# Decoder megakernel: context value products moved into the first stage's last rounds, one convolution product moved to GpSimd, and stage borders thinned

## The chip, the cores and the metric

The program runs on 1 core of one Trainium2 chip. The metric is the device time of one execution in microseconds (us); of several runs the median is taken. The engines are PE (TensorE, matmuls), DVE (VectorE), ACT (ScalarE), POOL (GpSimd) and SP (SyncE, which here only issues DMAs).

## The reference

Two decoder layers on x of 8 batches x 256 tokens x 512 features, with a context of the same shape, all in f32:

```python
x = _layernorm(x + _L0_attn_ref(x, ...), axis=-1)            # differential attention
x = _layernorm(x + _L0_xattn_ref(x, L0_xattn_k, fside_S2_0, ctx_2048, ctx_2048, 8), axis=-1)
x = _layernorm(x + _L0_ffn_ref(x, ...), axis=-1)             # 8 experts, top 2
x = _layernorm(x + _L1_attn_ref(x, ...), axis=-1)
x = _layernorm(x + _L1_xattn_ref(x, mask, ctx_2048, ctx_2048, wq, wk, wv, wo), axis=-1)
x = _layernorm(x + _L1_ffn_ref(x, W_gate, W_qkv), axis=-1)
```

Two pieces matter here. The long convolution of `_L0_xattn_ref` is, for each of the 32 groups of 8 channels, with v = x and x1 = x2 = context:

```python
kv = vr[:, :, :, None, :] * x2r[:, :, None, :, :]
y = jnp.fft.irfft(jnp.fft.rfft(kv, n=fft_size) * k_f[None, :, None, None, :], n=fft_size)[..., :L]
y = y + kv * skip
out = jnp.einsum('bhijl,bhil->bhjl', y, x1r)
```

And `_L1_xattn_ref` attends to the context, whose projections do not depend on x. The kernel folds the weights, so that the context is only multiplied by wq (scaled, "context queries", kept in DRAM as `ctx_q`) and by wo ("context values", `ctx_o`).

## The kernel before

The program is a sequence of stages, each a block with one hand-written instruction list per engine. A stage ends with `Stage.retire` (L44), which clears the stage's semaphores on POOL and puts up a barrier of all engines. Stages named `mid`, `kept` and `const` hold semaphores that live across the others, and each of them retires with a barrier too: `mid` before the last stage, `kept` and `const` at the end of the program. PSUM tiles are handed out in turn by `Banks` (L84): `claim` waits until the tile's turn before was drained, so a claim also waits for whoever drains the tile four turns back (the ring of the first stage has four).

**First stage (`front_stage`, L189).** Layer 0's attention, run as a software pipeline of rounds r = 0 to 11. In a round, batch d = r is projected, a = r-1 has its scores and exponentials, f = r-2 has the last part of its attention weighed, its output projection and norm, and u = r-3 is turned and gets its skip product. Rounds 2 to 8 hold all the work of a and f; in round 8 (a = 7) there is no d left, in round 9 (f = 7) no a either. PE's list is at L409 to L480. The score tiles (six `S` for the maxima, L310 to L330, six `T` for the exponentials, L344) share one buffer of four banks, so a score waits for the reader before it. The end of a round on the others:

- ACT (L671 to L681) takes the last exponential `exps(a, 5)`, copies the sums `take_sums(a, 1, 0)` (L607), and then makes `squares(a, 0)` (L611 and L612).
- POOL (L563 to L565) masks the last exponential tile (`causal(a, 5)`, L543, an affine select of 128x2048) and then adds the two squares (`add_eps(a, 0)`, L549), for which PE's `square_sums` (L380) of the next round waits.
- DVE's `combine(a, 1, 0)` (L720 to L725) needs ACT's sums; its last two operations read SBUF alone. After it come the maxima of the next round (`maxima`, L695), each of which releases PE's next score.

SP loads the inputs, stores `base` after each batch and, when T scores of batch 6 are made, loads the first two filters.

**Convolution (`long_conv_stage`, L893).** 32 groups h. POOL makes kv for the four chunks of 128 positions and the sum of the first two (L960, L958), into one of two buffers; it starts on h once PE has done with h-2. PE makes 9 products of 128x512 (L937), in f32, into 5 of 8 banks. DVE weighs the results with the context and sums over i: chunks 0 and 1 out of PSUM (L998), chunks 2 and 3 first completed with the shared part (L1004) and then, in SBUF, multiplied by the context (L1022); `sums` (L1009) reduces them two chunks at a time.

**Middle (`middle_stage`, L1033).** Norm, router, folding of weights, then routing on DVE (a long chain of small operations, in two pieces: up to the picks, and from the counts of L1182 to `hot_ready`), with PE filling the time with context products: for each batch `ctx_queries` (L1146) and `ctx_values` (L1154), batches 0 to 5. The counts come after batch 0's, the matmuls that make the token list (L1193) after batch 2's. After these POOL gathers the first two token tiles (L1246). ACT copies each result and stores it.

**Experts (`experts_stage`, L1411).** 39 tiles of 128 tokens: transpose (L1451), gate and up (L1456), silu, product, transpose, down (L1483), store. The first tile is transposed and copied (L1535) at the start. ACT ends by waiting for its stores, since the last stage gathers from them.

**Last stage (`tail_stage`).** Layer 1. It begins with the context products of batches 6 and 7.

## Time and profile before

| what | value |
|---|---|
| median of 3 runs | 2226.31 us (2226.2 to 2229.31) |
| the profiled execution, its own time | 2224.11 us |
| its span, first to last instruction | 2222.4 us |
| TensorE's mean granted clock | 0.979 |
| PE busy | 2093.0 us (94%) |
| DVE busy | 1250.0 us (56%) |
| POOL busy | 541.8 us (24%) |
| ACT busy | 516.3 us (23%) |
| DMA moved | 129.57 MB, 58 GB/s over the span |

Busy is the time in which an engine works on an instruction. Matmuls overlap, so the time that one matmul costs in a row of them is the distance of their starts. Where an engine idles, a row of the timeline tells how long and who released it.

### The profile page before, as it was taken

How to read it: one execution, taken by the hardware profiler on the slowest of the kernel's cores; microseconds unless marked ns; L12 is line 12 of the kernel's file. 1: busy time of each engine (PE TensorE's matmuls, PEld its weight loads, DVE VectorE, ACT ScalarE, POOL GpSimd, SP SyncE). 2: the span in 40 equal slices, each digit the busy share in tenths (PEclk: the TensorE clock that was granted, in tenths of full speed). 3: DMA queues.
4: the chain of work that ended last, by engine and by line, in shares of the span. 5: the costliest groups of instructions: out<-in, count | busy, mean ns of one | idle time of the engine just before them, and what ended most of it. 6: DMA issues, size and time to landing. Idle time of an engine off the chain costs nothing. (4 is left out here: it accounts for less than half of the span.)

```text
span 2222.4 us, 29341 instructions
## 1 busy us (share of the span) xinstructions
PE 2093.0 (94%) x11935; PEld 1221.2 (55%) x11935; DVE 1250.0 (56%) x1825; ACT 516.3 (23%) x783; POOL 541.8 (24%) x511
## 2 busy tenths in 40 slices
PE   7899999878999899899999898999999999999996
PEld 5444444324444466556665565566666666666654
DVE  2467777666999944022222225365757585847466
ACT  1444444440000121111111121122222222222121
POOL 2122222226777400011111221112121212111111
PEclk9999999989999999999999999999999999999998
DMA  8950000005111145521212412101010101000000
GB/s 171 99 48 29 29 29 20 31 10 200 46 42 42 34 140 190 200 67 62 67 67 67 178 40 96 48 1 48 1 58 1 58 1 39 1 29 11 1 10 20
DMA packets 65649, 129.57 MB, mean 58 GB/s; under 512 B 6416, under 2 KB 19856, under 8 KB 65520
## 3 DMA queue, kind: packets, MB, share of 16 engines
q1 hardware_dynamic: 44864, 75.39, 13.3%
q10 hardware_dynamic: 14976, 33.69, 4.2%
q0 software_dynamic: 5680, 18.62, 2.8%
q8 instruction: 99, 1.62, 0.3%
q14 instruction: 30, 0.25, 0.0%
HBM read 96.36 MB, written 41.81 MB: 62 GB/s over the span
## 5 line engine op out<-in xcount | busy, mean ns | idle before, releaser
L937 PE MATMUL conv_conv<-kv,toep 128*128 128x512 f32 x576 | 248.5, 594 | 0.0
L2434 DVE RECIPROCAL tail_inv<-tail_ring 128x256 f32<-128x256 f32 x64 | 112.4, 1756 | 188.7 <-PE tail_ring L1772 181.4
L1456 PE MATMUL moe_gu_ps<-gu,moe_xT 128*128 x624 | 199.0, 462 | 3.9 <-issue 2.3
L937 PEld LDWEIGHTS conv_conv<-kv,toep 128*128 128x128 f32 x576 | 110.0, 191 | 139.0 <-issue 131.6
L960 POOL TENSOR_TENSOR kv<-vT,cT 128x512 f32<-128x512 f32 x128 | 147.2, 1172 | 58.1 <-PE conv_conv L937 53.6
L1456 PEld LDWEIGHTS moe_gu_ps<-gu,moe_xT 128*128 128x128 f32 x624 | 116.0, 191 | 73.0 <-issue 23.6
L2125 POOL TENSOR_TENSOR tail_rstd_x<-tail_rstd_x,const_minus_half 128x2 f32<-128x2 f32 x31 | 21.9, 707 | 499.0 <-DVE tail_rstd_x L2386 499.0
L2132 POOL TENSOR_SCALAR_AFFINE_SELECT tail_expT<-tail_expT 128x1024 f32<-128x1024 f32 x64 | 71.2, 1112 | 237.3 <-ACT tail_expT L2207 237.1
L543 POOL TENSOR_SCALAR_AFFINE_SELECT front_expT<-front_expT 128x2048 f32<-128x2048 f32 x32 | 64.4, 2012 | 256.1 <-ACT front_expT L599 256.1
L1540 DVE TENSOR_TENSOR moe_hid<-moe_gu_ps,moe_silu 128x352 f32<-128x352 f32 x39 | 20.4, 524 | 179.3 <-PE moe_gu_ps L1456 179.3
L599 ACT ACTIVATE front_expT<-front_scores 128x2048 f32<-128x2048 f32 x48 | 90.1, 1878 | 81.1 <-PE front_scores L354 81.1
L2207 ACT ACTIVATE tail_expT<-tail_scores 128x1536 f32<-128x1536 f32 x64 | 92.8, 1450 | 66.3 <-PE tail_scores L1749 66.3
L1437 POOL DMA_INDIRECT xg<-x_after,tokens x37 | 34.9, 945 | 299.2 <-PE moe_xT_ps L1451 299.2
L1483 PE MATMUL moe_y_ps<-down,moe_hT 128*128 (+1 forms) x234 | 107.1, 593 | 0.7 <-ACT moe_hT L1524 0.7
L695 DVE TENSOR_REDUCE front_negtop<-front_scores 128x8 f32<-128x2048 f32 x32 | 73.2, 2288 | 27.8 <-PE front_scores L320 27.8
L2420 DVE TENSOR_TENSOR tail_allowed<-tail_scores,const_mask_bf 128x1024 f32<-128x1024 f32 x48 | 58.5, 1218 | 46.8 <-PE tail_scores L1724 46.6
L1022 DVE TENSOR_TENSOR total<-total,cT 128x512 f32<-128x512 f32 x62 | 82.8, 1374 | 1.1
L1507 ACT ACTIVATE moe_silu<-moe_gu_ps 128x352 f32<-128x352 f32 x39 | 18.1, 463 | 272.7 <-PE moe_gu_ps L1456 272.7
L2137 POOL TENSOR_TENSOR tail_expT<-tail_expT 128x512 f32<-128x512 f32 x60 | 76.6, 1277 | 5.0
L977 ACT COPY both<-conv_conv 128x512 f32<-128x512 f32 x32 | 18.6, 585 | 230.6 <-PE conv_conv L937 213.1
L1553 DVE COPY moe_y<-moe_y_ps 128x512 f32<-128x512 f32 x39 | 27.0, 691 | 72.4 <-PE moe_y_ps L1483 72.4
L185 PE MATMUL tail_ring<-tail_gk,tail_xT 128*128 128x416 f32 (+1 forms) x256 | 63.4, 399 | 3.3 <-ACT tail_xT L2190 3.3
(372 smaller groups left out, 4006.0 us busy)
## 6 DMA issues: line engine op xcount, KB each, us to landing
toep<-toeplitz SPq DMA_DIRECT2D x32, 320.0 KB, 2.9
y_slots<-moe_y ACTq DMA_DIRECT2D x39, 256.0 KB, 2.0
gu<-in_L_ffn_gate_up_proj SPq DMA_DIRECT2D x5, 1408.0 KB, 11.2
toeplitz<-filt_rows SPq DMA_DIRECT2D x1, 6144.0 KB, 66.7
front_e<-in_ctx SPq DMA_DIRECT2D x8, 512.0 KB, 5.5
toeplitz<-filt_rows SPq DMA_DIRECT2D x2, 2048.0 KB, 88.5
x_after<-x SPq DMA_DIRECT2D x8, 512.0 KB, 5.1
tail_x<-x_after SPq DMA_DIRECT2D x8, 512.0 KB, 4.0
```

Of the source, the lines that this page charges most:

```text
L543: pool.affine_select(out=tile, in_=tile, compare_op=ALU.is_ge, fill=0.0, base=0, pattern=[[0, 16], [1, P]], channel_multiplier=-1).then_in ...
L599: act.activation(exp_buf(b, n)[:].rearrange("p g j q -> p g (j q)"), scores[:], ACT.Exp).then_inc(quads.drained_sem(key), 1)
L695: ins = dve.tensor_reduce(negtop[:, 1, n].rearrange("p (g a) -> p g a", a=2), scores[:].rearrange("p g (a k) -> p g a k", a=2), AX_X, ALU. ...
L937: ins = pe.matmul(bank, toep[p][:, mat * P:(mat + 1) * P], kv[p][:, c].rearrange("p b j i -> p (b j i)"), start=n == 0, stop=n == len(PART ...
L960: pool.tensor_tensor(kv[p][:, c], tokens_of(c, h), context_of(c, h, 3), ALU.mult).then_inc(kv_ready, 1)
L1022: ins = dve.tensor_tensor(total[:, lc - 2], total[:, lc - 2], context_of(lc, h, 2), ALU.mult)
L1456: ins = pe.matmul(gu_ps[:, s % 2, h, 0:HID], xT[:, c, :], wgu[c][:, e, h * HID:(h + 1) * HID], start=c == 0, stop=c == NC - 1)
L1483: ins = pe.matmul(y_ps[:, s % 2, :], hT[0:w, n, :], wd[n][0:w, e, :], start=n == 0, stop=n == 2)
L2132: pool.affine_select(out=diagonal, in_=diagonal, compare_op=ALU.is_ge, fill=0.0, base=0, pattern=[[0, 8], [1, P]], channel_multiplier=-1). ...
L2137: pool.tensor_tensor(e[:, 3], e[:, 0], e[:, 2], ALU.add).then_inc(masked[kind], 1)
L2207: act.activation(exp_buf(kind, b, c)[:, 0:3].rearrange("p n g q -> p g n q"), scores[:, :, 0:3 * P].rearrange("p g (n q) -> p g n q", q=P) ...
L2434: link.after(dve.reciprocal(inv[c % 2][:], bank[:, S:2 * S]))
```

## The change

It has five parts.

1. **Context values of batches 0 to 2** leave the middle stage and are made in the first stage's rounds 8 and 9. There are six groups of four f32 products: batch 0 and the first half of batch 1 in round 8, the rest in round 9. Their weights (wo, 1 MB) are loaded by SP into `wq`, once the last query is projected; ACT copies and stores the results.
2. **Order in the first stage**, in every round: ACT squares before it copies the last sums; POOL adds before it masks the last tile; PE turns the context in two halves.
3. **Convolution**: POOL multiplies chunk 3 by the context (`weigh_last`), two groups late. DVE reduces chunk 2 and chunk 3 apart, chunk 3 one group late.
4. **First expert tile**: it is transposed in the middle stage, between the context queries and the context values of batch 5.
5. **Borders**: `mid`, `kept` and `const` retire without a barrier, and the wait for the experts' stores goes from ACT, ahead of the barrier, to POOL, behind it.

```diff
+        if not self.lasts:
+            self.nc.all_engine_barrier()
...
+                def ctx_values(b, t, parts=(0, 1)):
+                    key = ("ctxo", b, t)
+                    if 0 in parts:
+                        pe.wait_ge(ctx_wo_loaded, 16)
+                        ring.claim(pe, key)
+                    for c in range(NC // 2 * parts[0], NC // 2 * (parts[-1] + 1)):
+                        ins = pe.matmul(ring.tile(key), cT[:, b, c, t * P:(t + 1) * P], wide["wq"][:, c, :], start=c == 0, stop=c == NC - 1,
+                                        skip_group_check=True)
...
                         score(a, 0)
+                        if a == B - 1: ctx_values(0, 0, (0,))
                         if f is not None: square_sums(f, 0)
+                        if a == B - 1: ctx_values(0, 0, (1,))
...
-                        if f is not None: weigh(f, 1, 1, ("O",))
+                        if f is not None:
+                            weigh(f, 1, 1, ("O",))
+                            turn_context(f, 0)
...
-                            turn_context(f)
+                            turn_context(f, 1)
...
                         if u is not None: turn_tokens(u)
+                        if a == B - 1: ctx_values(0, 1, (0,))
...
                         if f is not None: square_sums(f, 1)
+                        if a == B - 1: ctx_values(0, 1, (1,))
                         score(a, 5)
+                        if a == B - 1: ctx_values(1, 0)
...
+                        ctx_values(1, 1)
                         weigh(f, 1, 1)
                         square_sums(f, 0)
                         turn_tokens(u)
+                        ctx_values(2, 0)
                         square_sums(f, 1)
                         octets(u)
                         for t in range(NT):
                             out(f, t)
+                        ctx_values(2, 1)
...
                     if a is not None:
+                        add_eps(a, 0)
                         causal(a, 5)
-                        add_eps(a, 0)
...
                     if a is None and u is not None:
                         for n in range(2):
                             take(("x1", u, n), vT[:, 2 * n:2 * n + 2, u, :])
+                    if a is None and f is not None: take_ctx_values(2, 0)
...
                         exps(a, 5)
+                        squares(a, 0)
                         take_sums(a, 1, 0)
-                        squares(a, 0)
...
+                def weigh_last(h):
+                    pool.wait_ge(ring.drained_sem((h, 3)), ring.count((h, 3)))
+                    pool.tensor_tensor(final[h % 2][:, 0], final[h % 2][:, 0], context_of(3, h, 2), ALU.mult).then_inc(weighed, 1)
...
+                        if h >= 2 and c == K01:
+                            weigh_last(h - 2)
+                weigh_last(H - 2)
...
+                    completed(h, 2)
+                    completed(h, 3)
+                    weighted_full(h, 2)
+                    sums(h, 2, total[:])
+                    if h:
+                        dve.wait_ge(weighed, h)
+                        sums(h - 1, 3, final[(h - 1) % 2][:])
+                weighted_full(H - 1, 3)
+                sums(H - 1, 3, final[(H - 1) % 2][:])
...
+                    if b == B - 3:
+                        pe.wait_ge(mid.gathered[0], 16)
+                        bank = ring.claim(pe, "tile")
...
+                    if b >= EARLY:
+                        ctx_values(b)
...
-                for p in range(2):
-                    act.wait_ge(y_stored[p], 16 * len(range(p, TILES, 2)))
...
+                for p in range(2):
+                    pool.wait_ge(y_stored[p], 16 * len(range(p, TILES, 2)))
                 fetch(0)
```

**Order on ScalarE, the end of a round of the first stage** (`expT` exponentials, `sums` the copied sums, `zz` and `square` the squares). Before:

```order
L599 ACTIVATE front_expT<-front_scores 128x2048 x2
L607 COPY front_sums<-front_ring 128x512
L599 ACTIVATE front_expT<-front_scores 128x2048
L607 COPY front_sums<-front_ring 128x512
L611 ACTIVATE front_zz<-front_zz 128x512
L612 ACTIVATE front_square<-front_am 128x512
```

Now:

```order
L627 ACTIVATE front_expT<-front_scores 128x2048 x2
L635 COPY front_sums<-front_ring 128x512
L627 ACTIVATE front_expT<-front_scores 128x2048
L651 ACTIVATE front_zz<-front_zz 128x512
L652 ACTIVATE front_square<-front_am 128x512
L635 COPY front_sums<-front_ring 128x512
```

The copy of the sums, for which DVE's combination waits, now stands behind both squares.

**Order on TensorE, from the end of round 8 into round 9** (`expT` with `v` and `ones` are the weighing, `front_e` is the turned context, `kept_wa` holds a batch of x that is turned, `front_wq` holds wo by then). Before:

```order
L373 MATMUL front_ring<-front_expT,front_v 32x512 x4
L373 MATMUL front_ring<-front_expT,front_ones 32x512 x4
L289 MATMUL front_ring<-const_ident,front_e 128x128 x8
L373 MATMUL front_ring<-front_expT,front_v 32x512 x8
L373 MATMUL front_ring<-front_expT,front_ones 32x512 x8
L380 MATMUL front_ring<-front_square,const_strips 128x512
L289 MATMUL front_ring<-const_ident,kept_wa 128x128 x8
L380 MATMUL front_ring<-front_square,const_strips 128x512
L394 MATMUL front_ring<-front_skipped,const_octets 128x512 x2
L387 MATMUL front_ring<-front_wo,front_am 128x512 x8
```

Now:

```order
L376 MATMUL front_ring<-front_expT,front_v 32x512 x4
L376 MATMUL front_ring<-front_expT,front_ones 32x512 x4
L292 MATMUL front_ring<-const_ident,front_e 128x128 x8
L406 MATMUL front_ring<-front_wq,cT 128x512 x4
L376 MATMUL front_ring<-front_expT,front_v 32x512 x8
L376 MATMUL front_ring<-front_expT,front_ones 32x512 x8
L383 MATMUL front_ring<-front_square,const_strips 128x512
L292 MATMUL front_ring<-const_ident,kept_wa 128x128 x8
L406 MATMUL front_ring<-front_wq,cT 128x512 x4
L383 MATMUL front_ring<-front_square,const_strips 128x512
L397 MATMUL front_ring<-front_skipped,const_octets 128x512 x2
L390 MATMUL front_ring<-front_wo,front_am 128x512 x8
```

One group of context values stands ahead of the weighing of f = 7, one ahead of its second square sums.

**Order on TensorE in the middle stage, behind the last logits** (`midl_ring<-cT,plain_wq` queries, `raw_wo,cT` values, `marked` the token list). Before:

```order
L1146 MATMUL midl_ring<-cT,plain_wq 128x256 x16
L1154 MATMUL midl_ring<-raw_wo,cT 128x512 x8
L1182 MATMUL midl_count_ps<-m,earlier 128x128
L1182 MATMUL midl_count_ps<-m,ones 128x128
L1146 MATMUL midl_ring<-cT,plain_wq 128x256 x16
L1154 MATMUL midl_ring<-raw_wo,cT 128x512 x8
L1146 MATMUL midl_ring<-cT,plain_wq 128x256 x16
L1154 MATMUL midl_ring<-raw_wo,cT 128x512 x8
L1193 MATMUL midl_ring<-marked,at_lane 128x78 x32
L1146 MATMUL midl_ring<-cT,plain_wq 128x256 x16
L1154 MATMUL midl_ring<-raw_wo,cT 128x512 x8
L1146 MATMUL midl_ring<-cT,plain_wq 128x256 x16
```

Now:

```order
L1215 MATMUL midl_ring<-cT,plain_wq 128x256 x16
L1250 MATMUL midl_count_ps<-m,earlier 128x128
L1250 MATMUL midl_count_ps<-m,ones 128x128
L1215 MATMUL midl_ring<-cT,plain_wq 128x256 x48
L1223 MATMUL midl_ring<-raw_wo,cT 128x512 x8
L1268 MATMUL midl_ring<-marked,at_lane 128x78 x32
L1215 MATMUL midl_ring<-cT,plain_wq 128x256 x16
L1223 MATMUL midl_ring<-raw_wo,cT 128x512 x8
L1215 MATMUL midl_ring<-cT,plain_wq 128x256 x16
L1259 MATMUL midl_ring<-const_ident,xg_73 128x128 x4
L1223 MATMUL midl_ring<-raw_wo,cT 128x512 x8
```

Three pairs of value groups are gone; the counts stand behind one batch of queries, the token list behind 4 of queries and 1 of values; the transposes of the first tile (`xg`) come before the last values.

## Rows read from the trace of the kernel before

**Rows 1.** Engines by stretch (us, busy (x instructions), clock): a round, last rounds, convolution
```profile
253.00:309.00 56.00, 53.91 (x368) 26.38 (x368) 39.73 (x48) 26.64 (x36) 11.50 (x8) 1.00 0.09 29
...
421.00:478.00 57.00, 46.80 (x300) 17.25 (x300) 35.94 (x42) 20.28 (x23) 10.37 (x7) 0.91 0.03 10
...
514.00:768.00 254.00, 248.57 (x577) 109.69 (x575) 241.65 (x259) 18.62 (x32) 183.10 (x157) 0.99 0.22 73
```

**Rows 2.** Timeline of TensorE in the middle stage: start us, us, what [idle before]
```profile
842.75 7.03 PE L1154 MATMUL midl_ring<-raw_wo,cT 128*128 128x512 f32 x16
849.62 0.38 PE L1182 MATMUL midl_count_ps<-m,earlier 128*128 128x128 f32 x2
...
913.32 7.03 PE L1154 MATMUL midl_ring<-raw_wo,cT 128*128 128x512 f32 x16
```

**Rows 3.** Timeline of TensorE and VectorE where the expert stage begins
```profile
922.83 1.09 PE L1451 MATMUL moe_xT_ps<-const_ident,xg 128*128 128x128 f32 x4 [2.48 <-PEq L52]
926.20 6.54 PE L1456 MATMUL moe_gu_ps<-gu,moe_xT 128*128 x16 [2.29 <-issue]
...
932.86 0.53 DVE L1540 TENSOR_TENSOR moe_hid<-moe_gu_ps,moe_silu 128x352 f32<-128x352 f32 x1 [8.22 <-PE moe_gu_ps L1456]
```

**Rows 4.** Landing of the gathers, from the view of tile xg
```profile
DMA to landing us min/median/max: 3.2/3.3/8.1
```

**Rows 5.** Timelines of ScalarE, GpSimd, VectorE, TensorE where round 6 begins
```profile
306.30 0.59 ACT L607 COPY front_sums<-front_ring 128x512 f32<-128x512 f32 x1
...
308.32 1.43 POOL L549 TENSOR_TENSOR front_square<-front_square,front_zz 128x512 f32<-128x512 f32 x1
...
308.55 1.48 DVE L725 SCALAR_TENSOR_TENSOR front_am<-front_cross,front_lam 128x256 f32<-128x256 f32 x1
309.96 2.28 DVE L695 TENSOR_REDUCE front_negtop<-front_scores 128x8 f32<-128x2048 f32 x1
...
309.80 1.12 PE L380 MATMUL front_ring<-front_square,const_strips 128*128 128x512 f32 x2 [1.10 <-POOL front_square L549]
...
316.65 0.61 PE L316 MATMUL front_scores<-const_mask_bf,const_ident_bf 128*128 128x256 bf16 x4 [0.63 <-DVE front_negtop L695]
```

**Rows 6.** Timeline of TensorE in round 9 and into the convolution
```profile
480.46 1.92 PE L373 MATMUL front_ring<-front_expT,front_v 128*32 128x512 f32 x16 [2.30 <-DVE front_cross L722]
...
490.10 2.08 PE L380 MATMUL front_ring<-front_square,const_strips 128*128 128x512 f32 x2 [3.74 <-POOL front_square L549]
...
507.06 1.97 PE L289 MATMUL front_ring<-const_ident,kept_wvo 128*128 128x128 f32 x8 [4.41 <-DVE kept_wvo L783]
510.53 3.75 PE L928 MATMUL conv_conv<-front_e,const_octets 128*128 128x512 f32 x4 [1.50 <-PEq L52]
```

**Rows 7.** Timelines of GpSimd and VectorE, end of round 8; all of L725
```profile
476.09 2.24 POOL L543 TENSOR_SCALAR_AFFINE_SELECT front_expT<-front_expT 128x2048 f32<-128x2048 f32 x1
...
476.39 2.22 DVE L725 SCALAR_TENSOR_TENSOR front_am<-front_cross,front_lam 128x256 f32<-128x256 f32 x1
...
L725 DVE SCALAR_TENSOR_TENSOR front_am<-front_cross,front_lam x32: 471/478/2223, 72.1 to 486.0; 128x256 f32<-128x256 f32 x32
```

**Rows 8.** Convolution: three operations by line; timelines of GpSimd (608) and VectorE (767)
```profile
L960 POOL TENSOR_TENSOR kv<-vT,cT x128: 1062/1067/2049, 510.5 to 751.6; 128x512 f32<-128x512 f32 x128
...
L958 POOL TENSOR_TENSOR kv<-kv x32: 1263/1271/1276, 512.7 to 749.4; 128x512 f32<-128x512 f32 x32
...
L1022 DVE TENSOR_TENSOR total<-total,cT x62: 677/1328/1554, 529.2 to 759.2; 128x512 f32<-128x512 f32 x62
...
608.15 2.09 POOL L960 TENSOR_TENSOR kv<-vT,cT 128x512 f32<-128x512 f32 x2 [1.79 <-PE conv_conv L937]
...
767.01 0.69 DVE L1009 TENSOR_REDUCE vT<-total 128x64 f32<-128x512 f32 x1
```

**Rows 9.** Timeline of TensorE where the last stage begins
```profile
1249.60 0.67 PE L1846 MATMUL tail_ring<-cT,plain_wq 128*128 128x256 f32 x2 [4.00 <-PEq L52]
```

**Rows 10.** Timeline of SyncE's queue at the end
```profile
2217.29 1.34 SPq L2107 DMA_DIRECT2D out_x<-tail_x  x2
```

149 lines of the change are left out of this document (91 added, 58 removed).

## The prediction

> **What bounds the kernel now.** I read the page first: PE is busy for 94% of the span and heads the chain that ended last, so a microsecond counts only if it lies on PE's path. The engines by stretch then show where PE is the limit [rows 1]. A round of the first stage takes 56 us, PE is busy for 53.91 of them. In the last rounds it idles for 10.2 of 57 us at a granted clock of 0.91. In the convolution it is busy for 248.57 of 254 us; DVE has 241.65 and POOL 183.10. A group there is 248.5 / 32 = 7.77 us of PE work. The middle stage and the experts run without PE idle in a row of matmuls. So three things can move the time: products that PE no longer makes in a full stretch, PE's idle at a border or a late round, and another engine that becomes the bound. The rest is hidden.
>
> All sums are against the profiled execution, 2224.11 us. It lies 2.2 us below the median of 2226.31 us, and I add these 2.2 us at the end.
>
> **(a) Three batches of values out of the middle.** 16 recorded matmuls take 7.03 us, and the next work begins 849.62 - 842.75 = 6.87 us after the first of them [rows 2]. PE is full there, so 3 x 6.87 = 20.6 us go. What could give some back: the routing chain on DVE and the gathers run behind this work. The counts now come behind one batch of queries, without the 6.87 us of values, so the routing starts earlier by that. From counts to token list there were four pieces of 6.87 us before (two batches of queries and values) and there are four now. From the list to the first use of the gathered tile three pieces remain, 20.6 us, and the slowest gather took 8.1 us to land [rows 4]. So: -20.6.
>
> **(b) First expert tile.** Before, the last values ended at 913.32 + 6.87 = 920.2 us and the first gate matmul began at 926.20: 6.0 us, made of a border (2.48), 1.09 of transposes and 2.29 of waiting for their copy and the expert's number [rows 3]. Now the transposes stand in the middle stage: two 128x128 matmuls took 0.38 [rows 2], so four of two passes about 0.7. The border of 2.5 stays, and I leave 1.4 of the 2.29, since the number must still be read. That is 4.6 us against 6.0: -1.4. The SiLU waits for the last store of context results, which hardly moves towards it: its product began right behind the up matmuls at 932.86 [rows 3], so little slack is there. Bounds: 0 and -3.4.
>
> **(c) The order in rounds 2 to 7.** ACT now squares first, POOL adds first. The add began at 308.32 and PE's square sums at 309.80, after 1.10 us of idle [rows 5]. With the squares ahead of the copy (0.59), and the add ahead of the select (2.24 [rows 7]), this idle goes. But DVE's combination waits for the copy, which comes later by two squares, about twice 0.6, as the copy itself (0.59) has as many elements: 1.2 us. It then meets POOL's select instead of the shorter add. What that does rows 7 show: beside a select of 2.24 us the last operation of the combination took 2.22 us, against a median of 0.478. Beside the add of 1.43 us it took 1.48 [rows 5]: it ends some 0.28 us behind POOL's operation both times (310.03 against 309.75; 478.61 against 478.33). I place the new select at about 308.7 to 310.7, so the combination ends at 311.3 and the maxima at 311.3 + 2.28 = 313.6, where they ended at 309.96 + 2.28 = 312.24. The next score waits for them (PE idled 0.63 for the same reason at 316.65 [rows 5]). Of the 1.3 us the earlier square sums and the halved turning of the context absorb part; I take +0.8 a round, +4.8 for six rounds. Bounds: -6.6 (the idle of 1.10 goes, nothing comes) and +9 (1.5 a round).
>
> The Trainium skill (SBUF — State Buffer, "SBUF: two separate sides") says that GpSimd and VectorE share a port pair under an exclusive lock, held for the whole instruction. By that rule alone the delay would be the select's rest, up to 2.2 us a round, or +13; without it the step would bring -6.6. The stretched operations of rows 5 and 7 agree with it.
>
> **(d) Rounds 8, 9 and the convolution's start.** Six value groups of 3.44 us (half of 6.87) enter, 20.6 us of work. Three go into round 8, where PE idles for 10.2 us [rows 1]: their 10.3 us fill the idle, and some slow matmuls there run at full clock: -1.3. In round 9 (1,1) goes ahead of the weighing, whose start waited 2.30 for DVE, and delays it by about 2.4, since its tile was only just drained by then. (2,0) lies in the 3.74 of idle before the second square sums at 490.10 [rows 6], but ACT takes (2,0) ahead of the squares. With the 2.4 this moves the square sums to about 494.8, +4.65. What stands behind them (2.08 in rows 6, then octets and output projection) runs at a higher clock, which I put at -1.15: the norm ends +3.5 later. (2,1) lies in the 4.41 us of idle ahead of the last turning. That turning took 1.97 for 8, though 8 of the same shape take half of that at full clock, the four of L928 took 3.75 where full clock needs about half [rows 6], and the first products were slow too: 1.0 + 1.8 + 1.1 = 3.9 come back. Together -1.3 + 3.5 - 3.9 = -1.7. This is my least certain term: bounds -8 (the moved sums cost nothing, and the clock is back) and +6 (ACT's delay and the 2.4 in full, no clock). Loading wo (1 MB) and ACT's extra stores lie beside this, where SP and ACT idle, and cost nothing.
>
> **(e) The convolution.** PE's 32 x 7.77 us stay. DVE loses a product of 1.33 us median a group [rows 8], which shortens an engine that was hidden. POOL idled 1.79 us before a group [rows 8]. Its new weighing is not in the trace; nearest are its products of the same size in two groups of lines, 1.067 us (L960) and 1.27 us (L958, all in SBUF), the longest 2.05. I take 1.27, as its input too was just written in place: POOL has 7.73 - 1.79 + 1.27 = 7.2 us in a group of 7.73 and stays hidden, with 0.5 us left. Only at the end, where DVE drains behind PE, one product less counts, less a sum (0.69) that now stands apart: -0.8.
>
> The Trainium skill (Perfetto Trace Analysis, "Optimizing Scalar/DVE Operations") warns that moving work between GpSimd and DVE may not help, for their shared port. By it the 1.33 us are not gained; here they aren't counted anyway. The spread of L1022 (0.68 to 1.55) [rows 8] agrees.
>
> **(f) Experts to the last stage.** PE begins at 1249.60 after 4.00 us [rows 9], against 2.48 at the border before the experts [rows 3]. The difference, 1.5, is the wait for the stores, which POOL now takes while PE starts its own context work; the barrier of `mid` goes too, 0.6 at least: -2.1. Bounds -3 and 0.
>
> **(g) The end.** `kept` and `const` retire without a barrier. The last store was issued by 2217.29 + 1.34 = 2218.6 [rows 10], the span ends at 2222.4; landing takes about 2 of these 3.8 us (the page's median for the experts' stores). Two barriers can be 0 to 2: -1.0.
>
> **The sum:** -20.6 - 1.4 + 4.8 - 1.7 - 0.8 - 2.1 - 1.0 = -22.8, so 2224.11 - 22.8 = 2201.3, and 2203.5 for the median.
>
> **The rivals.**
> 1. The order in the rounds helps: the combination isn't caught, and 1.10 goes in each of six rounds, -6.6 in place of +4.8: about 2192. For it speaks PE's idle before the square sums, against it both stretched rows. 0.12.
> 2. The last rounds cost more: (d) at +6 in place of -1.7, as ACT's copies delay squares, every tile of the ring of four waits for its drain, and the moved groups delay PE instead of filling its idle: 7.7 more, about 2211. For it speaks that ACT and DVE, not PE, set round 9. 0.15.
> 3. The middle gives back 5 us, because gathers or expert weights are late: about 2208.5. Against it stand 20.6 us of cover over 8.1. 0.07.
> 4. The other side: POOL becomes the bound of the convolution. The weighing would have to exceed 1.79 us to bind at all; to make up for 22.8 us and 4.5 more, the group must grow by 27.3 / 31 = 0.88 us, so the weighing must take over 2.67 us. By the longest row, 2.05, it costs only 0.26 x 31 = 8 us (2211.5). At 3.0 us, if each weighing waits in full for a DVE product and each DVE product for POOL, it is 1.21 x 31 = 37 us: 2241, slower than before. For it: both engines would be busy for nearly the whole group. Against: the median of L960 is its minimum nearly, although DVE is 95% busy beside it. 0.04.
>
> **How the numbers follow.** Forecast 0.62, rivals 0.12, 0.15, 0.07, 0.04. The range goes from 2195 (three quarters of the way to rival 1) to 2211 (rival 2). A measurement of this kernel can tell about 0.2%, 4.5 us, from no change. Faster by more: all but rival 4 and a tail, 0.94; within 0.2%: 0.03; slower: 0.03.
>
> **What the profile would show.** (a) PE's middle stage shorter by 20 us and without new idle before the transposes. (b) The first gate matmul about 4.6 us behind the last values. (c) Rounds of 56.8 us, combinations stretched to some 2 us, no idle before the square sums and more before the next score; rounds of 55 would prove me wrong. (d) Clock near 1 from round 8 on, idle before the second square sums of round 9. (e) 32 groups of 7.7 us, POOL busy for 7.2 of them, with idle for PE; if POOL has none, rival 4 holds. (f), (g) PE's first matmul of the last stage some 2.5 us behind the experts, and a shorter end. A time above 2211 or below 2195 would say that a step is missing.

## Result and the profile after

The changed kernel takes 2205.7 us (2201.74 to 2211.74, 4 runs) against 2227.74 us for the kernel before (2226.2 to 2229.31, 4 runs): a ratio of 0.9902, 95% interval 0.9881 to 0.9923. That is 22.0 us less, where 22.8 were forecast, and the time lies in the range. The near hit hides errors that cancel, though, as the stretches show. In a second set of runs the same kernel had a median of 2209.39 (2202.33 to 2214.41, 6 runs) and the kernel before 2227.01 (2219.94 to 2231.49, 11 runs): 17.6 us less there, and either kernel moves by some 12 us between executions.

The page's busy line of after:

```profile
PE 2088.7 (95%) x11935; PEld 1215.9 (55%) x11935; DVE 1203.7 (55%) x1825; ACT 516.0 (23%) x783; POOL 578.7 (26%) x542
```

TensorE is busy for 4.3 us less (it has the same products to make) and its mean granted clock is 0.984 (0.979 before); VectorE's work fell by 46 us and GpSimd's grew by 37.

The profiled execution after is 2205.38 us, its span 2203.6, which is 18.8 less than before. I cut both spans at the same seven places of TensorE's timeline (start of the first square sums of round 2, of round 7, of the first convolution product, the first matmul of the middle stage, the first context queries, the first gate matmul, the first matmul of the last stage):

| stretch | before | after | difference | forecast |
|---|---|---|---|---|
| start to the square sums of round 2 | 84.85 | 79.49 | -5.36 | -1.1 |
| five rounds | 280.84 | 288.78 | +7.94 | +4.0 |
| rounds 7 to 9, to the convolution | 148.39 | 153.56 | +5.17 | +0.2 |
| convolution and its border | 254.34 | 252.05 | -2.29 | -0.8 |
| middle, up to the queries | 67.34 | 66.99 | -0.35 | 0 |
| queries to the first gate matmul | 90.44 | 68.42 | -22.02 | -22.0 |
| experts and their border | 323.40 | 322.16 | -1.24 | -2.1 |
| last stage to the end | 972.80 | 972.15 | -0.65 | -1.0 |

(The forecasts are the terms of the prediction by stretch; the square sums come 1.1 earlier in their round, which is -1.1 in the first row and comes back in the third.) The first row is no effect of the change: of the 14 profiles of this study, before's among them, the granted clock of the first 80 us is 0.89 in six and 0.96 in eight, with kernels of the old and of the changed order in either group, and the square sums of round 2 come at 84.1 to 85.4 or at 79.0 to 81.3 us.

The routing and middle stage, columns as in [rows 2]: TensorE's timeline after.

```profile
847.86 0.38 PE L1250 MATMUL midl_count_ps<-m,earlier 128*128 128x128 f32 x2
...
897.83 0.60 PE L1259 MATMUL midl_ring<-const_ident,xg 128*128 128x128 f32 x4
898.27 7.03 PE L1223 MATMUL midl_ring<-raw_wo,cT 128*128 128x512 f32 x16
909.29 3.29 PE L1540 MATMUL moe_gu_ps<-gu,xT_tile 128*128 x5 [3.99 <-issue]
```

No matmul of the middle stage waits for the routing, and the transposes of the first tile have no idle ahead of them: the three batches of values ([rows 2]) are gone in full. The gate begins 909.29 - (898.27 + 6.87) = 4.15 us behind the last values, where it was 6.0. But its first 16 matmuls took 7.42 us here and 6.54 before ([rows 3]): TensorE's idle is now one piece of 3.99 us, and from 909 to 912 us the granted clock was 0.50. In a second profile of the same kernel (e0 below) they took 6.69 us. So 0.9 us of the 1.4 gained at this border went to the clock in this profile, which is most of why the experts' row has -1.24 and not -2.1.

A round of the first stage, the one that answers to [rows 5]: TensorE, then VectorE, GpSimd and ScalarE.

```profile
253.52 1.10 PE L383 MATMUL front_ring<-front_square,const_strips 128*128 128x512 f32 x2
...
258.25 0.61 PE L319 MATMUL front_scores<-const_mask_bf,const_ident_bf 128*128 128x256 bf16 x4 [1.91 <-DVE front_negtop L743]
258.79 2.09 PE L323 MATMUL front_scores<-front_kT,front_qT 32*128 32x512 f32 x8
260.80 2.62 PE L376 MATMUL front_ring<-front_expT,front_v 128*32 128x512 f32 x16
...
253.41 2.19 DVE L772 TENSOR_TENSOR front_zz<-front_sums 128x256 f32<-128x256 f32 x1
255.91 2.28 DVE L743 TENSOR_REDUCE front_negtop<-front_scores 128x8 f32<-128x2048 f32 x1
...
252.09 1.27 POOL L577 TENSOR_TENSOR front_square<-front_square,front_zz 128x512 f32<-128x512 f32 x1 [5.69 <-ACT front_square L652]
253.31 2.00 POOL L571 TENSOR_SCALAR_AFFINE_SELECT front_expT<-front_expT 128x2048 f32<-128x2048 f32 x1
...
251.91 0.58 ACT L635 COPY front_sums<-front_ring 128x512 f32<-128x512 f32 x1
```

ScalarE's copy of the sums now ends at 252.49. GpSimd's select began at 253.31 and ended at 255.31. VectorE's multiplication of the sums (L772, SBUF alone), which takes 0.426 us at the median, took 2.19 and ended at 255.60, 0.29 behind it: it is the forecast pile-up, one operation earlier than placed. Without it the combination would have ended 1.8 us sooner, so the select, and not the later copy alone, makes it late. The maxima then end at 258.19, and PE, which before had idled 1.10 and 0.63 us in two places [rows 5], idles 1.91 in one. Behind that idle the next matmuls are slow: L323 took 2.09 us here, 1.14 one score later.

The granted clock of that place, in the engines by stretch (as in [rows 1]: the stretch, its length, then busy time of PE, its weight loads, VectorE, ScalarE and GpSimd, the granted clock, and DMA share and GB/s):

```profile
256.00:259.00 3.00, 1.09 (x10) 0.53 (x12) 3.00 (x2) 0.38 (x1) 0.00 (x0) 0.97 0.00 0
259.00:262.00 3.00, 3.00 (x16) 0.70 (x20) 1.86 (x2) 0.00 (x0) 0.00 (x0) 0.50 0.00 0
...
314.00:317.00 3.00, 1.09 (x10) 0.46 (x11) 3.00 (x3) 0.38 (x1) 0.00 (x0) 1.00 0.00 0
317.00:320.00 3.00, 3.00 (x26) 0.81 (x27) 2.78 (x2) 0.00 (x0) 0.00 (x0) 1.00 0.00 0
```

In the first of the two rounds the clock was granted at 0.50 for three microseconds (1.2 GHz), right after the idle; in the next round the same idle left it at 1.00. A round with the fall lasted 58.09 us (253.52 to 311.61), one without it 56.66, before 55.89. So the order, with the halved turning, costs 0.77 a round, as forecast (0.8), and where the clock falls another 1.43, which was not forecast.

The last rounds, answering to [rows 6], TensorE, ScalarE, and the engines by stretch:

```profile
482.72 3.67 PE L406 MATMUL front_ring<-front_wq,cT 128*128 128x512 f32 x8 [1.40 <-DVE front_cross L770]
492.07 3.60 PE L406 MATMUL front_ring<-front_wq,cT 128*128 128x512 f32 x8
498.80 2.08 PE L383 MATMUL front_ring<-front_square,const_strips 128*128 128x512 f32 x2 [3.12 <-POOL front_square L577]
515.79 1.09 PE L292 MATMUL front_ring<-const_ident,kept_wvo 128*128 128x128 f32 x8 [0.98 <-DVE kept_wvo L831]
518.43 3.56 PE L980 MATMUL conv_conv<-front_e,const_octets 128*128 128x512 f32 x4 [1.55 <-PEq L52]
...
495.77 0.60 ACT L602 ACTIVATE front_xT<-front_ring 128x512 f32<-128x512 f32 x1 [2.21 <-PE front_ring L406]
496.26 0.62 ACT L651 ACTIVATE front_zz<-front_zz 128x512 f32<-128x512 f32 x1
...
511.00:514.00 3.00, 3.00 (x8) 1.33 (x7) 2.39 (x7) 0.00 (x0) 0.01 (x1) 1.00 0.00 0
519.00:522.00 3.00, 3.00 (x5) 1.18 (x4) 0.69 (x1) 0.00 (x0) 2.92 (x4) 0.56 0.66 195
```

ScalarE's squares (from 496.26) stood behind its copy of the values (2,0) (495.77), which waits for PE to finish that group at 495.7. The second square sums then waited 3.12 us for GpSimd, and behind this idle they ran at the lower clock (2.08 us for a pair that takes 1.12 in round 9's first sums). So did the round's octets right behind them (3.62 for 4; 1.88 in e2 below, where the idle is gone). The output projection ran at full clock but for its start (7.29 for 16, 7.13 in e2), and the clock stood at 1.00 until the convolution's border. There it fell anew: the convolution's octets took 3.56 for 4. In e0, the same kernel with the same waits (3.13 and 1.55), they took 1.95 at full clock:

```profile
521.45 1.95 PE L980 MATMUL conv_conv<-front_e,const_octets 128*128 128x512 f32 x4 [1.55 <-PEq L52]
```

So the octets' slowness is not the square sums' doing, and why it comes in one execution and not in the other is open. The products behind the octets did get faster, as forecast: the first twelve came within 6.44 us here and 7.57 before, a gain of 1.1 us that lies in the convolution's row of the table.

GpSimd's weighing (L1005) and products in the convolution, by line (ns: least, median, most), answering to [rows 8]:

```profile
L1005 POOL TENSOR_TENSOR final<-final,cT x31: 1260/1267/1649, 537.0 to 762.3; 128x512 f32<-128x512 f32 x31
L1016 POOL TENSOR_TENSOR kv<-vT,cT x128: 1055/1066/2047, 518.4 to 759.9; 128x512 f32<-128x512 f32 x128
```

And the timeline of GpSimd in one group, of TensorE at the two borders and of SyncE at the end ([rows 8, 9, 10]):

```profile
630.22 2.53 POOL L1016 TENSOR_TENSOR kv<-vT,cT 128x512 f32<-128x512 f32 x2 [0.57 <-PE conv_conv L989]
634.06 1.27 POOL L1005 TENSOR_TENSOR final<-final,cT 128x512 f32<-128x512 f32 x1
...
773.88 3.30 PE L1176 MATMUL midl_ring<-const_ident,vT 128*128 128x128 f32 x16 [4.69 <-PEq L52]
...
1231.45 4.73 PE L1927 MATMUL tail_ring<-cT,plain_wq 128*128 128x256 f32 x13 [1.92 <-PEq L52]
...
2199.16 1.33 SPq L2188 DMA_DIRECT2D out_x<-tail_x  x2
```

The convolution in the engines by stretch, the third of [rows 1] again:

```profile
514.00:768.00 254.00, 251.47 (x588) 111.43 (x587) 192.53 (x258) 20.31 (x35) 226.07 (x192) 0.99 0.24 77
```

The weighing takes the 1.267 us that were forecast; GpSimd still idles 0.57 us a group (1.79 before), and PE's rate in the groups is unchanged.

### The profile page after: what moved, and what is told of

The parts are those of the page before. It is cut to its first block and busy times, and to the rows that moved or that the text cites. A ratio compares the mean times of both kernels' runs of the same rounds, so it can differ in the third digit from the quotient of the medians.

```text
span 2203.6 us, 29354 instructions
## 1 busy us (share of the span) xinstructions
PE 2088.7 (95%) x11935; PEld 1215.9 (55%) x11935; DVE 1203.7 (55%) x1825; ACT 516.0 (23%) x783; POOL 578.7 (26%) x542
## 5 line engine op out<-in xcount | busy, mean ns | idle before, releaser
L989 PE MATMUL conv_conv<-kv,toep 128*128 128x512 f32 x576 | 247.4, 592 | 0.0
L1540 PE MATMUL moe_gu_ps<-gu,xT_tile 128*128 x624 | 199.9, 464 | 5.6 <-issue 4.0
L1540 PEld LDWEIGHTS moe_gu_ps<-gu,xT_tile 128*128 128x128 f32 x624 | 116.5, 192 | 75.5 <-issue 26.5
L2290 ACT ACTIVATE tail_expT<-tail_scores 128x1536 f32<-128x1536 f32 x64 | 92.8, 1450 | 67.4 <-PE tail_scores L1830 67.3
L178 PE MATMUL front_ring<-front_xT,front_wq 128*128 128x256 f32 x256 | 61.6, 390 | 2.0 <-ACT front_wq L668 2.0
```

What stands on the lines that cost most here:

```text
L178: ins = pe.matmul(out, w[:, c, col:col + n], xT[:, c, :], start=c == 0, stop=c == NC - 1)
L989: ins = pe.matmul(bank, toep[p][:, mat * P:(mat + 1) * P], kv[p][:, c].rearrange("p b j i -> p (b j i)"), start=n == 0, stop=n == len(PART ...
L1540: ins = pe.matmul(gu_ps[:, s % 2, h, 0:HID], xT[:, c, :], wgu[c][:, e, h * HID:(h + 1) * HID], start=c == 0, stop=c == NC - 1)
L2290: act.activation(exp_buf(kind, b, c)[:, 0:3].rearrange("p n g q -> p g n q"), scores[:, :, 0:3 * P].rearrange("p g (n q) -> p g n q", q=P) ...
```

## The experiments

All are edits of the changed kernel. They ran on three chips: e0 to e3 on one, e4, e6, e7 and e8 on the second, e5, e9, e10 and e12 on the third. The kernel before had medians of 2227.01, 2229.08 and 2226.97 us there. Stretches of the profiles, cut at the same places: the start up to the square sums of round 2, five rounds, rounds 7 to 9, the convolution, the experts with their border, and the last stage. The start depends on the clock as said above (0.96 where it is 79 to 81). Of the two stretches left out, the first one of the middle stage is 67.0 to 67.4 us throughout but for e0 and e9 (70.05).

| kernel | median us | start | rounds | 7 to 9 | conv. | experts | last |
|---|---|---|---|---|---|---|---|
| before | 2227.01 | 84.85 | 280.84 | 148.39 | 254.34 | 323.40 | 972.80 |
| e0 changed, again | 2209.39 | 79.96 | 290.29 | 152.99 | 252.42 | 321.46 | 972.67 |
| e1 old order | 2201.19 | 85.44 | 284.32 | 150.85 | 252.40 | 321.44 | 972.77 |
| e2 late copy | 2202.76 | 78.98 | 286.23 | 149.26 | 252.41 | 321.47 | 972.57 |
| e3 convolution back | 2207.48 | 80.34 | 290.26 | 152.99 | 253.59 | 322.62 | 976.38 |
| e4 no move | 2230.47 | 84.06 | 287.37 | 154.11 | 252.71 | 322.45 | 972.70 |
| e5 old order, late copy | 2192.47 | 84.81 | 279.43 | 145.60 | 252.41 | 321.44 | 972.49 |
| e6 the same, waits filled | 2192.08 | 80.40 | 281.70 | 145.97 | 252.41 | 321.43 | 972.78 |
| e7 idle split | 2202.83 | 80.14 | 283.13 | 152.57 | 252.05 | 322.24 | 972.61 |
| e8 as e6, changed order in round 8 | 2193.18 | 81.29 | 281.21 | 146.67 | 252.05 | 322.20 | 972.18 |
| e9 as e6, all barriers | 2196.84 | 85.37 | 279.50 | 145.96 | 252.42 | 321.44 | 973.50 |
| e10 as e6, convolution back | 2197.95 | 80.84 | 284.15 | 147.66 | 253.57 | 322.69 | 976.44 |
| e12 as e6, changed order | 2200.42 | 84.36 | 284.81 | 147.35 | 252.41 | 321.43 | 972.72 |

**e0_after**, no edit.

> The changed kernel once more, beside the others of this call. Its first profile has rounds of the first stage of 58.1 us where the granted clock fell at the round's start (four of six) and of 56.7 us where it did not. Theory A (the fall hangs on the single idle of 1.9 us of PE, and comes or not by chance): again a mix of 56.7 and 58.1, time 2200 to 2212. Theory B (the fall belonged to that chip or execution): no round of 58.1.

Ratio to before 0.9918 (0.9896 to 0.994). From round 3 to round 7 each fell: the square sums come at 137.85, 195.96, 254.06, 312.16, 370.25 and 429.35 us, 58.1 apart (the last one, with half a value group in it, 59.1 against 57.7). Theory A's mix didn't show within this profile, but over the two the same round lasted 56.66 or 58.1, and theory B is out. That the idle is what lets the clock fall is not shown by this run.

**e1_old_order**:

```diff
-                        add_eps(a, 0)
                         causal(a, 5)
+                        add_eps(a, 0)
...
-                        squares(a, 0)
                         take_sums(a, 1, 0)
+                        squares(a, 0)
```

> The changed kernel with the old order on ScalarE (sums, then squares) and GpSimd (select, then add); the two halves of the context stay. Theory A (the combination waits for the select on the shared port, which costs 0.8 us in each of six rounds, and the idle gathered in one place lowers the clock for another 1.4 in four of them): rounds of 55.9 us or less, 10 us less in all, about 2195. Theory B (the rounds' length came from the clock alone, by chance): no change, about 2205. Theory C (the new order pays, since the square sums come earlier): slower, up to 2212.

2201.19 us, ratio 0.9878 (0.9856 to 0.99), 8.2 less than e0 on the same chip (the intervals just touch). Four rounds in a row lasted 55.59 to 55.64 us, a little under before's 55.89; PE's only other difference there is the halved turning. Theory A holds for the rounds. (Both pairs were swapped back at once, so what each of the two swaps is worth alone is not shown.) It doesn't hold for round 9: from the last exponential's scores to the second square sums it took 25.3 us, where the changed order takes 22.7. The old order makes the tile of (1,1) come free 0.9 us later, and behind that idle the matmuls were slow:

```profile
481.99 5.37 PE L406 MATMUL front_ring<-front_wq,cT 128*128 128x512 f32 x8 [2.31 <-DVE front_cross L770]
499.76 1.86 PE L383 MATMUL front_ring<-front_square,const_strips 128*128 128x512 f32 x2 [3.12 <-POOL front_square L577]
```

The group of 8 took 5.37 us where 3.67 is its length at full clock. This isn't a fixed price: in e5, behind the same idle (2.30), it took 3.67.

**e2_take_late**:

```diff
-                    if a is None and f is not None: take_ctx_values(2, 0)
...
                         squares(f, 1)
+                        if a is None: take_ctx_values(2, 0)
```

> The changed kernel with ScalarE's copy of the context values (2,0) behind the last squares of round 9, not ahead of them. Theory A (that copy's wait for PE holds the squares): the second square sums come 2.7 us earlier behind the last exponential than the 21.7 us of the first profile, and the kernel is 2 to 3 us faster, about 2203. Theory B (TensorE's tiles or the combination decide there): no change.

2202.76 us, ratio 0.9898 (0.9876 to 0.9921), 6.6 less than e0, though the intervals of the two overlap. The profile is clear, in TensorE's timeline and in the engines by stretch:

```profile
494.37 1.13 PE L383 MATMUL front_ring<-front_square,const_strips 128*128 128x512 f32 x2 [0.32 <-POOL front_square L577]
512.68 1.96 PE L980 MATMUL conv_conv<-front_e,const_octets 128*128 128x512 f32 x4 [1.55 <-PEq L52]
```

```profile
494.00:518.00 24.00, 19.87 (x51) 8.59 (x50) 17.41 (x26) 4.36 (x7) 6.28 (x6) 1.00 0.26 98
```

The sums waited 0.32 instead of 3.12 us and came 2.8 us earlier in their round (19.87 behind the last exponential's scores, 22.67 in the changed kernel), as theory A had it. With the idle gone the clock stayed at 1.00 from there to the convolution. The stretch is 3.7 us shorter than e0's: 2.8 of the wait, and 0.9 behind it, where e0 ran its sums and round 9's octets slower. The convolution's octets (L980) have no part in this, they took 1.95 us in e0 too.

**e3_conv_back**: GpSimd's `weigh_last` and the two `final` buffers out, VectorE's products as in the kernel before.

```diff
-                        if h >= 2 and c == K01:
-                            weigh_last(h - 2)
-                weigh_last(H - 2)
...
+                        for lc in (2, 3):
+                            ins = dve.tensor_tensor(total[:, lc - 2], total[:, lc - 2], context_of(lc, h, 2), ALU.mult)
+                        link.after(ins)
+                        sums(h, 2, 2)
```

> The changed kernel with the convolution's products as before: VectorE weighs chunk 3 too, GpSimd does not. Theory A (PE bounds the convolution either way, and only the drain at its end and a little at its start change): slower by 1.2 to 2.3 us, about 2207.5, groups of 7.7 us both ways. Theory B (GpSimd's products hold up VectorE or PE): faster. Theory C (VectorE, 95% busy, held PE back before): slower by 4 us or more.

2207.48 us, ratio 0.9916 (0.9894 to 0.9938), no difference from e0 by the medians. In the profile the convolution's stretch is 253.59 against 252.42 us, +1.17, and all of it lies behind the last product:

```profile
777.18 3.65 PE L1165 MATMUL midl_ring<-const_ident,vT 128*128 128x128 f32 x16 [5.87 <-PEq L52]
```

PE idled 5.87 us there, 5.85 before, and 4.69 after (773.88 above). PE's work from the first product to the last took 247.7 us in both e0 and e3. Theory A; C is out: VectorE at 95% held nobody up, and taking a product off it is worth its drain alone. (This profile, 2213.97 us, is 6.5 above the run's own median; 3.7 of that is a slower last stage, see e10.)

**e4_no_move**: `EARLY = 0`, no value groups in the first stage, values of batch 0 ahead of the counts and the token list behind batch 2, as before.

```diff
-EARLY = 3
+EARLY = 0
...
-                        ctx_values(2, 0)
                         square_sums(f, 1)
...
-                        ctx_values(2, 1)
...
                 ctx_queries(0)
+                ctx_values(0)
                 pe.wait_ge(shaped, 1)
...
-                    if b == EARLY:
+                    if b == 2:
```

> The changed kernel with all six batches of context values in the middle stage as before, and none in the first stage; order, convolution, first tile and borders stay as changed. Theory A (the six groups cost 3 to 4 us in rounds 8 and 9, where PE idled or ran at half clock, and save 20.6 in the middle): slower than the changed kernel by 17 us, about 2224, close to the kernel before. Theory B (a part of the 20.6 is hidden elsewhere, or the groups cost 8 or more in the first stage): slower by 12 or less, about 2219.

2230.47 us, ratio to the kernel before 1.0011 (0.9999 to 1.0022). Both theories are off: against 2209.39 and 2205.7 the move alone is worth 21 to 25 us, and all the rest of the change together nothing. The stretch from the queries to the gate is 88.86 us, 20.4 more than with the move, as computed. But the stretch of rounds 7 to 9 didn't get shorter without the groups: 154.11 against 152.99 and 153.56 with them. The six groups cost less than nothing there. Two waits show where PE stood without them:

```profile
432.82 1.04 PE L319 MATMUL front_scores<-const_mask_bf,const_ident_bf 128*128 128x256 bf16 x4 [3.71 <-DVE front_negtop L724]
433.79 2.09 PE L323 MATMUL front_scores<-front_kT,front_qT 32*128 32x512 f32 x8
...
490.18 3.64 PE L376 MATMUL front_ring<-front_expT,front_v 128*32 128x512 f32 x16 [3.30 <-POOL front_expT L560]
493.57 3.19 PE L376 MATMUL front_ring<-front_expT,front_ones 128*32 128x512 f32 x16
...
488.07 2.01 POOL L560 TENSOR_SCALAR_AFFINE_SELECT front_expT<-front_expT 128x2048 f32<-128x2048 f32 x1
```

PE waited 3.71 us for the maxima in round 8, and 3.30 for GpSimd's select ahead of the last weighing, since the select now stands behind the add; each time the next matmuls ran at half clock (3.64 for 16 that take 1.92). In the kernel before the idle was 1.71 and 1.36 us at the first place, with slow matmuls behind it too, and 2.30 at the second, with none. So without the groups the changed order costs nearly 4 us in the last rounds, with the clocks as they were in these two profiles: 154.11 - 148.39, less 0.8 of round 7 and 1.1 by which the mark at its start is earlier. The groups fill the holes that it makes: with them the two orders differ by less than 0.3 us from the square sums of round 8 to the first product (89.69 in e12, 89.96 in e5).

**e7_split_idle**:

```diff
                             query(d, 0)
+                        if f is not None: turn_context(f, 0)
                         score(a, 1)
                         if f is not None:
                             weigh(f, 1, 1, ("O",))
-                            turn_context(f, 0)
```

> The changed kernel, but PE turns the first half of the context ahead of the second score, inside the 1.9 us in which it waits for the maxima, not behind the first weighing. Theory A (what lowers the clock at the round's start is this idle in one piece; 1.4 us of it are then left): no round of 58.1 us, rounds of 56.2, about 2200. Theory B (the clock falls all the same, since the path over VectorE is as long): rounds of 58 at a lowered clock still, no gain, about 2207.

2202.83 us, ratio 0.9895 (0.9871 to 0.9919). Rounds 3 to 6 lasted 56.67 us and none fell, but none lasted 56.2 either:

```profile
252.59 0.60 PE L292 MATMUL front_ring<-const_ident,front_e 128*128 128x128 f32 x4
254.66 0.61 PE L319 MATMUL front_scores<-const_mask_bf,const_ident_bf 128*128 128x256 bf16 x4 [1.47 <-DVE front_negtop L743]
258.83 0.61 PE L319 MATMUL front_scores<-const_mask_bf,const_ident_bf 128*128 128x256 bf16 x4 [0.63 <-DVE front_negtop L743]
```

The idle of 1.47 us has a second one of 0.63 behind it: what PE does in the wait is not gained, as VectorE's maxima set the pace. Whether splitting the idle prevents the fall isn't settled. e2 has 1.9 us in one piece and four rounds of 56.67 without a fall too, and the 6 runs here still spread from 2199.82 to 2210.82.

**e6_fill_gaps**, on e1's and e2's edits:

```diff
+                        if f is not None: turn_context(f, 0)
                         if f is not None: square_sums(f, 0)
...
                             weigh(f, 1, 1, ("O",))
-                            turn_context(f, 0)
+                            turn_context(f, 1)
...
                             weigh(f, 1, 1, ("Z",))
-                            turn_context(f, 1)
```

> Old order on ScalarE and GpSimd, ScalarE's late copy of (2,0), and the two halves of the context in PE's two waits at the head of a round: one ahead of the first square sums, one between the first weighing and the third score. Theory A (these waits are free time, the halves cost nothing there): rounds of 55.2 us against 55.6, round 9 as with the late copy, about 2194. Theory B (VectorE sets the round's length from the maxima on, so that what PE saves it waits for later): rounds of 55.6, about 2197. Theory C (a new wait for a tile): slower.

2192.08 us (2191.63 to 2192.61, 5 runs), ratio 0.9839 (0.9816 to 0.9861): faster than both kernels. Rounds of 55.60 us, as theory B said (but for round 3, 57.86, with a pause of 2.09 us that no releaser explains); TensorE's timeline, and the engines by stretch over round 9:

```profile
250.90 1.12 PE L383 MATMUL front_ring<-front_square,const_strips 128*128 128x512 f32 x2 [0.52 <-POOL front_square L577]
261.84 0.61 PE L319 MATMUL front_scores<-const_mask_bf,const_ident_bf 128*128 128x256 bf16 x4 [0.56 <-DVE front_negtop L743]
```

```profile
470.00:515.00 45.00, 38.05 (x132) 16.17 (x133) 30.85 (x43) 12.32 (x21) 14.39 (x13) 1.00 0.25 87
```

What was filled ahead of the sums (0.52 left of 1.10) comes back as 0.56 ahead of the fourth score. Rounds 7 to 9 take 145.97 us, 2.4 less than before although they do 20.6 us more of matmuls, at a clock of 1.00.

**e5_old_order_take_late**, e1's and e2's edits alone:

> The fastest version so far (2192.1) without the filled waits: the halves of the context stand as in the changed kernel, the order is the old one, the copy of (2,0) late. Theory A (rounds were 55.6 us with and without the filling in the profiles; what the filling gives is that the clock no longer falls at the head of a round): runs from 2193 to 2200 with a median near 2196, where the filled version's spread is 1 us. Theory B (the filling gave nothing): 2192, spread as small.

2192.47 us (2191.26 to 2200.9), ratio 0.9852 (0.9827 to 0.9878). The median is e6's, four runs lie at 2191.3 to 2193.7 and two at 2196.7 and 2200.9. So the filling is not shown to be worth anything; that it makes falls rarer (5 of 5 runs of e6 within 1 us, 4 of 6 here within 2.4) is a hint and no more. In the profiles it was e6 that had a long round and e5 that had none. The gain belongs to the order and the late copy.

**e8_old_but_last**, e6 with the changed order in round 8 only, on GpSimd and likewise on ScalarE:

```diff
+                        if a == B - 1: add_eps(a, 0)
                         causal(a, 5)
-                        add_eps(a, 0)
+                        if a < B - 1: add_eps(a, 0)
```

> As the run that fills the two waits, but in round 8, where no further scores follow, the changed order of squares, sums, add and select. Theory A (there the earlier combination's tile frees PE sooner: PE waited 1.4 us for the tile of (1,1) with the changed order and 2.3 with the old, which also lowered the clock): 0.9 to 2.6 us faster than with the old order throughout, about 2192. Theory B (no difference, PE's wait there is hidden by the weighing's own): same as with the old order.

2193.18 us (2192.05 to 2195.38), ratio 0.9845 (0.9822 to 0.9867): no difference from e6. Round 9's waits are shorter (sums to sums 62.79 against 63.70), the convolution starts 0.7 us later in its stretch all the same, on slower octets (3.40 us from the first of them to the first product, 1.79 in e6). Theory A's gain is given back by slower octets, which the kernel before, e4, e7 and the first profile of the changed kernel have too and for which no cause is shown.

**e9_barriers**, on e6:

```diff
-        if not self.lasts:
-            self.nc.all_engine_barrier()
+        self.nc.all_engine_barrier()
```

> The fastest version so far (2192.1: old order, late copy of (2,0), filled waits) with a barrier again wherever a stage, mid, kept or const retires. Theory A (the trace of the changed kernel has 0.7 us less behind the last store, and of the 2.1 us gained ahead of the last stage most is the stores' wait that went to GpSimd, not the barrier): slower by 1.2 to 1.6 us, about 2193.5. Theory B (the barriers overlap the last store's landing): no change.

2196.84 us (2192.72 to 2205.31), ratio 0.9866 (0.984 to 0.9893). The profile is more use than the median. Ahead of the last stage nothing changed (321.44 against 321.43), at the end there is 0.72 more (973.50 against 972.78). The other microseconds are the clock of the start (0.89) and of the middle stage (a stretch of 70.05 against 67.35), which e0 shows as well. So the barrier of `mid` was free; by elimination the 2.08 us gained there belong to the stores' wait that went to GpSimd. No run puts that wait back.

**e10_fill_conv_back**, e6 with e3's edit:

> The fastest version so far (2192.1) with the convolution as before: VectorE weighs chunk 3. Theory A (PE bounds the groups, only the drain at the end is 1.2 us longer, 5.9 against 4.7 from PE's last product to its first of the middle stage): 2193.3. Theory B (GpSimd's share of the port does cost elsewhere): 2192 or less.

2197.95 us (2195.11 to 2202.93), ratio 0.9865 (0.9843 to 0.9888). The convolution's stretch is 1.16 us longer, as in e3. The median is 5.9 higher, on another chip. The profile can't divide that, since its execution (2202.93) lies 5.0 above the run's median. Of the 10.7 us between its span and e6's, 4.6 are the start and the rounds up to the convolution, 1.3 the experts and 3.7 the last stage, which took 976.44 us instead of 972.78 (in e3 976.38) with instructions that are the same. The engines by stretch, from 75 to 175 us into that stage, e10 and then e6:

```profile
1300.00:1400.00 100.00, 87.68 (x536) 49.68 (x535) 47.70 (x79) 17.76 (x26) 20.80 (x20) 0.91 0.20 66
```

```profile
1293.00:1393.00 100.00, 87.59 (x553) 51.12 (x552) 51.35 (x85) 18.53 (x27) 20.84 (x20) 0.97 0.21 69
```

The clock there is 0.91 against 0.97. e3 and e10 have it and no other kernel of this study, the kernel before with the same convolution (972.80) included. The edit doesn't touch that stage; why the clock falls there in these two stays open, and so does whether the runs that were not profiled have it.

**e12_fill_new_order**, e6 with the changed order on ScalarE and GpSimd:

> The fastest version so far (2192.1) with the changed order on ScalarE and GpSimd: the order is the only difference. Theory A (the select catches the combination): rounds of 56.7 against 55.6 us, 6 us slower, with falls of the clock on top, 2198 to 2205. Theory B (with the waits filled the order no longer matters): 2192.

2200.42 us (2196.15 to 2204.45), ratio 0.988 (0.9856 to 0.9903): 8.3 us slower than e6 and 8.0 than e5, which ran on the same chip. Rounds of 56.67 us against 55.60:

```profile
255.25 2.19 DVE L772 TENSOR_TENSOR front_zz<-front_sums 128x256 f32<-128x256 f32 x1
260.10 0.61 PE L319 MATMUL front_scores<-const_mask_bf,const_ident_bf 128*128 128x256 bf16 x4 [1.52 <-DVE front_negtop L743]
```

The combination is stretched to 2.19 us again and PE waits 1.52 for the maxima. No round fell in this profile, so 1.07 x 6 = 6.4 us is the part that the pile-up costs without the clock. e5's profile, whose start has the same clock (0.89), reaches the convolution's first product 6.7 us sooner (509.84 against 516.52). Against e6's profile the difference is 8.5, but 4.0 of that is the start. Theory A.

## Why the prediction was right, and where it was wrong

(a) and (b), the move and the first tile: 22.0 forecast, 22.02 measured. Routing, gathers and weights stayed hidden. The first tile's part was 6.0 - 4.15 - 0.44 (the transposes' place in the middle stage, 897.83 to 898.27) = 1.4, as forecast up to the gate; 0.9 of it was lost behind the gate's start to the clock, a term that the prediction didn't have.

(c), the order: +0.8 a round forecast, +0.77 measured, and by the mechanism named. The Trainium skill (SBUF — State Buffer, "SBUF: two separate sides") has the shared port locked for a whole instruction; the trace agrees, with VectorE's operation ending 0.29 us behind the select, and the cost is less than the select's length because only the part behind 253.41 is waited for. The halves gave 0.28 of it back already (old order, 55.61 against 55.89), so the order itself costs 1.07 (e12). What the step lacked is the clock: the pile-up gathers PE's idle in one place, and behind it the clock fell in three of rounds 3 to 7 of this profile and in all five of e0's, 1.43 us each. That made five rounds +7.94 (forecast +4.0).

(d), rounds 8 and 9, is the step that failed: -1.7 forecast. The table's +5.17, less 0.77 for round 7 and 1.1 for the shifted mark, is +3.3, and with the 1.1 us that the first products gave back in the convolution's row it is +2.2. What failed is the clock that was to come back. The square sums came 0.9 us later than placed, and behind their wait, which I had seen, the clock fell once more, so that nothing of the 1.15 up to the norm came (16.96 us from these sums to the last turning before, 16.99 after). "The four of L928 ... full clock needs about half" was to return 1.8 us and returned 0.2 (3.75 to 3.56). The turning (1.97 to 1.09) and the first products (1.1) did come as forecast. The octets' term is chance in part, since in e0 they ran at full clock: there (d) is +0.6, the fall in round 7 taken out. And I costed ScalarE's copy by its delay alone; taking it away was worth 3.7 us (e2), 2.8 of wait and the rest clock. I also had not asked what the order does in the last rounds, where less work hides it: e4 puts that at nearly 4 us without the groups, e12 and e5 at nothing with them. The groups themselves are free, even a little better than that.

(e) GpSimd's weighing: forecast 1.27, measured 1.267 us, idle left 0.5 and 0.57. The gain at the drain was 1.17 against 0.8. The other 1.1 of that stretch is PE's time in the groups, 248.5 before and 247.4 after. All of it lies in the first twelve products, and e3, with the convolution of before, has 247.7 as e0 has, so it is the clock at the start, which (d) had counted, and not GpSimd. (f) -2.1 and -2.08 (1242.76 to 1249.60 before, 1226.69 to 1231.45 after, both from the start of the last products); but the barrier's share of 0.6 was nothing (e9). (g) -1.0 forecast, -0.65 and -0.72 measured, inside its bounds.

The sum of the profiles is -18.8 against -22.8. (c) and (d) missed by 3.9 each, the clock behind the gate by 0.9; the clock of the start, which belongs to neither kernel, made good for 4.3 of it, and small misses in the other stretches for 0.4. The medians differ by 22.0 because the profiled execution before (2224.11) was 3.6 faster than the median of its runs. The total was right partly by luck; (a), (b) up to the gate and (e) were right by their steps. (f) was right in its sum, but its barrier term was wrong and the wait for the stores correspondingly larger than the 1.5 forecast.

The rivals: the first (the order helps) is refuted by e1 and e12. The second (the last rounds cost more, through ScalarE's copy) is in part what happened in these rounds, at +2.2 instead of +6: ScalarE's copy did delay the squares, the groups did not delay PE. The third did not occur. The fourth needed a weighing of 2.67 us; the longest was 1.65.

## What to carry to other kernels

An order that lets one engine start 1.1 us sooner can cost more than that on the engine beside it: look which of the two shares a resource with the long operation that is being moved. A wait of PE costs more than its length when the matmuls behind it run at half clock: 1.43 us on top of 1.9 here, and not in every execution. Where variants differ by a few microseconds, compare the same stretch of two profiles beside the medians, and look at the granted clock of that stretch first: of the eleven profiles with the changed convolution seven agree there within 0.02 us (252.40 to 252.42), where two medians of one kernel differ by 4. One profile can't explain a median from which its own execution lies 5 us away.

## What the runs showed of the hardware

The granted clock of the first 80 us came out at one of two values (0.89, 0.96) in profiles of much the same program, worth 4 to 5 us. Kernels that differ by 1 us of work differed by 6 in the median (e6 and e10, on two chips). The runs of e6 agree within 1 us, those of its near copies don't; why is open. Whenever one of the combination's last two operations, which work on SBUF alone, was held by an operation of GpSimd, it ended 0.27 to 0.29 us behind that one. That holds in all 14 profiles, for either of the two and for the select as for the add. In the kernel before both were caught in each round, one by the select and one by the add, and in the changed one only the first, for longer. The kernel before, VectorE and GpSimd (its add and the stretched L725 are in [rows 5]):

```profile
307.80 0.83 DVE L724 TENSOR_TENSOR front_zz<-front_sums 128x256 f32<-128x256 f32 x1
476.05 0.42 DVE L724 TENSOR_TENSOR front_zz<-front_sums 128x256 f32<-128x256 f32 x1
...
306.35 2.00 POOL L543 TENSOR_SCALAR_AFFINE_SELECT front_expT<-front_expT 128x2048 f32<-128x2048 f32 x1 [4.65 <-ACT front_expT L599]
```

The prediction did not have the first of these (0.83 us where 0.43 is the median). The combination's first two operations, which also read PSUM, were never stretched (at most 0.426 us, beside GpSimd's add too). GpSimd's own select took 2.00 us in the changed rounds, so it is VectorE that waits there. In the kernel before the select of [rows 7] began 0.04 us after an L724 had (476.09 against 476.05); that L724 took its usual 0.424 us and the select 2.24, so the engine that began later was the one that waited.
